# A weight-rounding pass in whole steps of 1024 columns, and xT casts on another engine, in an attention and feed-forward layer

## The reference

```python
# attention: 16 heads of 64
scores = q @ k^T * hs ** -0.5
p = softplus(scores) ** 2 * causal
out = (p / (sum(p, -1) + 1e-9)) @ v
x = layernorm(x + out @ w_proj^T + b_proj)

# feed-forward, d = 1024, f = 4096
def fake_quant_weight(w):
    scale = max(abs(w)) / 127
    return clip(round(w / scale), -128, 127) * scale
def qat_lora_linear(x, W, b, A, B):
    return x @ fake_quant_weight(W)^T + b + 2 * ((x @ A^T) @ B^T)
h = gelu(qat_lora_linear(x, W_fc, b_fc, A_fc, B_fc))
x = layernorm(x + qat_lora_linear(h, W_proj, b_proj, A_proj, B_proj))
```

## Time and profile before

| | us |
|---|---|
| median of 2 runs | 5843.04 |
| lowest and highest run | 5838.0, 5848.07 |
| the profiled execution | 5820.75 |
| its span, slowest core (core 7) | 5819.2 |
| spans of the 8 cores | 5794.4 to 5819.2 |

### The profile page before, as it was taken

One profiled execution on the slowest core, in us unless ns is written; L12 is line 12 of the kernel. 1 busy time (PEld: TensorE's weight loads), 2 busy tenths in 40 slices (PEclk: granted clock), 3 DMA queues, 4 the chain that ended last, 5 costly groups with the idle time before them and its releaser, 6 DMA issues. The chain is left out here.

```text
span 5819.2 us, 51500 instructions; the slowest of 8 cores (5794.4 to 5819.2 us)
## 1 busy us (share of the span) xinstructions
PE 3331.9 (57%) x12354; PEld 1140.0 (20%) x12354; DVE 1985.1 (34%) x3426; ACT 1831.0 (31%) x2257; POOL 233.0 (4%) x246
## 2 busy tenths in 40 slices
PE   0464555655665555556656620111478979888897
PEld 0121111111002211111110000000134434444343
DVE  2224333333333243333333345888821010111101
ACT  0005464655760053636647710000011111111111
POOL 0000101000001001010000000000000000000000
PEclk9975656555557856565555555555678888888888
DMA  3210101000001101010000025111100000000000
GB/s 83 78 57 14 48 9 48 6 7 33 5 6 52 58 20 50 9 47 7 7 33 5 6 89 183 55 56 56 62 15 30 15 30 15 15 30 15 30 15 15
DMA packets 91382, 205.94 MB, mean 35 GB/s; under 512 B 16823, under 2 KB 17080, under 8 KB 91100
## 3 DMA queue, kind: packets, MB, share of 16 engines
q1 hardware_dynamic: 81820, 169.09, 9.5%
q0 software_dynamic: 9280, 33.56, 1.4%
HBM read 168.79 MB, written 33.82 MB: 35 GB/s over the span
## 5 line engine op out<-in xcount | busy, mean ns | idle before, releaser
L551 DVE TENSOR_TENSOR a_p<-a_ph 128x1024 bf16<-128x1024 bf16 x640 | 445.4, 696 | 1319.5 <-ACT a_ph L548 1207.1
L543 ACT ACTIVATE a_tE<-psA 128x1024 f32<-128x1024 f32 x640 | 654.8, 1023 | 536.3 <-PE psA L533 505.7
L979 PE MATMUL psA<-b_Wp,b_h 128*128 128x512 bf16 x2048 | 581.5, 410 | 413.7 <-DVE b_Wp L816 392.1
L548 ACT ACTIVATE a_ph<-a_tE 128x1024 bf16<-128x1024 f32 x640 | 676.1, 1056 | 61.8 <-DVE a_p L551 2.8
L533 PE MATMUL psA<-a_Q,a_K 64*128 64x512 bf16 x1280 | 633.7, 596 | 2.2 <-DVE a_Q L474 2.2
L579 PE MATMUL psO<-a_p,a_V 128*65 128x512 bf16 x640 | 331.8, 621 | 519.0 <-DVE a_p L551 311.8
L579 PE MATMUL psU<-a_p,a_V 128*65 128x512 bf16 x640 | 315.0, 593 | 511.3 <-DVE a_p L551 272.6
L951 ACT ACTIVATE b_h<-psO,g_bfccol 128x256 bf16<-128x256 f32 x256 | 121.2, 473 | 1030.9 <-PE psO L943 1029.5
L1007 DVE TENSOR_SCALAR b_u<-psU 16x256 bf16<-16x256 f32 x16 | 6.6, 412 | 1106.3 <-PE psU L987 1106.3
L935 PE MATMUL psO<-b_X1T,b_Wfc 128*128 128x256 bf16 x2048 | 304.6, 298 | 89.2 <-DVE b_Wfc L816 76.6
L405 PE MATMUL psA<-a_xT,a_wqkv 128*128 128x512 bf16 x512 | 128.7, 418 | 335.6 <-POOL a_xT L309 335.6
(11 more groups left out here) (97 smaller groups left out, 3027.9 us busy)
## 6 DMA issues: line engine op xcount, KB each, us to landing
g_wstg<-xT SPq DMA_DIRECT2D x128, 256.0 KB
a_xf<-x SPq DMA_DIRECT2D x32, 512.0 KB
g_bc<-recb SPq DMA_DIRECT2D x128, 128.0 KB
x1scr<-g_xo POOLq DMA_DIRECT2D x32, 512.0 KB, 3.8
b_ws<-wfcT SPq DMA_DIRECT2D x32, 512.0 KB
b_ws<-wpF SPq DMA_DIRECT2D x32, 512.0 KB
b_x1f<-x1scr SPq DMA_DIRECT2D x32, 512.0 KB
b_ws<-wfcT SPq DMA_DIRECT2D x64, 256.0 KB
```

The costliest lines, as they stand in the source:

```text
L543: ve = kb.op("scalar", lambda E, pp=pp: E.activation(a_tE[:, :], psA[:, pp * 1024:(pp + 1) * 1024], AF.Exp, scale=0.125), waits=[(sPE, sco ...
L548: vl = kb.op("scalar", lambda E: E.activation(a_ph[:, :], a_tE[:, :], AF.Ln, bias=1.0), waits=[(sDV, st.get("ph_sq", 0))], inc=sAC)
L551: vsq = kb.op("vector", lambda E, pp=pp: E.tensor_tensor(a_p2[:, pp * 1024:(pp + 1) * 1024], a_ph[:, :], a_ph[:, :], ALU.mult), waits=[(sA ...
L979: kb.op("tensor", lambda E, q=q, tc2=tc2, oh=oh, pp=pp, f=f: E.matmul(psA[:, q * 512:(q + 1) * 512], b_h[:, pp * 256 + tc2 * 128: pp * 256 ...
```

## The change

It has two parts.

1. The second pass works on whole pieces. `emit_p2_step` takes the place of `emit_p2_half` and `halves`: one load of 128x1024 f32 (512 KB) into one of the two slots of `b_ws`, and the same seven instructions on 1024 columns, in `b_d`, `b_zi` and `b_r` from column 0. There are 64 steps in the same order: 8 of `b_Wfc`, 4 of `b_Wp`, three times, then 8 and the last 20. A load waits for the first operation of the step that used its slot before. The gates stand at the same places of the work.
2. The loads of xT for keys and values go through `load_xT`, so that VectorE does the 8 x 8 casts (before: GpSimd). The matmuls wait for VectorE's count. `load_xT_pool` stays for the queries of the later blocks, without its second argument.

```diff
-                    xtg_t = load_xT_pool(base + tg * 512, extra_waits=w + xw)
+                    xtg_ready = load_xT(base + tg * 512, extra_waits=w + xw)
                     for kf in range(CC):
                         bank = kf % 4
-                        w = [xtg_t, (sDV, st["psA_free"][bank])]
+                        w = [(sDV, xtg_ready), (sDV, st["psA_free"][bank])]
...
-            ws_free2 = [(sDV, ws_free[0]), (sDV, ws_free[0]),
-                        (sDV, ws_free[1]), (sDV, ws_free[1])]
-            qst = {"d_free": [0, 0], "rfin": [0, 0], "qi": 0, "first": True}
+            ws_free2 = [(sDV, ws_free[0]), (sDV, ws_free[1])]
+            qst = {"qi": 0, "first": True}
...
+            def emit_p2_step(which, src, dst, n):
                 sc = 4 * which
+                slot = qst["qi"] % 2
                 qst["qi"] += 1
+                vd = kb.dma("sync", lambda E, src=src, slot=slot, n=n: E.dma_start(
+                    out=b_ws[:, slot * 1024: slot * 1024 + n], in_=src),
+                    waits=[ws_free2[slot]])
+                wq = [vd]
                 if qst["first"]:
                     wq.append(scl_ready)
                     qst["first"] = False
+                vz = kb.op("vector", lambda E, slot=slot, n=n, sc=sc: E.tensor_scalar(
+                    b_d[:, 0:n], b_ws[:, slot * 1024: slot * 1024 + n],
                     g_scl[:, sc + 1:sc + 2], None, ALU.mult),
                     waits=wq, inc=sDV)
+                ws_free2[slot] = (sDV, vz)
+                kb.op("vector", lambda E, n=n: E.tensor_copy(
+                    b_zi[:, 0:n], b_d[:, 0:n]))
+                kb.op("vector", lambda E, n=n: E.tensor_copy(
+                    b_r[:, 0:n], b_zi[:, 0:n]))
+                kb.op("vector", lambda E, n=n: E.tensor_tensor(
+                    b_d[:, 0:n], b_d[:, 0:n], b_r[:, 0:n], ALU.subtract))
+                kb.op("vector", lambda E, n=n: E.scalar_tensor_tensor(
+                    b_r[:, 0:n], b_d[:, 0:n], 0.5, b_r[:, 0:n],
+                    ALU.is_ge, ALU.add))
+                kb.op("vector", lambda E, n=n: E.scalar_tensor_tensor(
+                    b_r[:, 0:n], b_d[:, 0:n], -0.5, b_r[:, 0:n],
+                    ALU.is_ge, ALU.add))
+                vfin = kb.op("vector", lambda E, dst=dst, n=n, sc=sc: E.tensor_scalar(
+                    dst, b_r[:, 0:n], g_scl[:, sc + 2:sc + 3],
                     g_scl[:, sc + 3:sc + 4], ALU.mult, ALU.add), inc=sDV)
                 return vfin
...
-                    for _ in range(16):
-                        vfin = emit_p2_half(0, *wfc_halves[fi])
+                    for _ in range(8):
+                        vfin = emit_p2_step(0, *wfc_steps[fi])
                         fi += 1
                     qfc_gate[hh] = vfin
-                    nwp = 8 if hh < 3 else 40
+                    nwp = 4 if hh < 3 else 20
                     for _ in range(nwp):
-                        if pi >= 64:
+                        if pi >= FC:
                             break
-                        vfin = emit_p2_half(1, *wp_halves[pi])
+                        wp_gate[pi] = emit_p2_step(1, *wp_steps[pi])
                         pi += 1
-                        if pi % 2 == 0:
-                            wp_gate[pi // 2 - 1] = vfin
```

More of the change, by code:

```diff
@@ L297, in load_xT, with load_xT_pool @@
                 return last
-            def load_xT_pool(t0, extra_waits=()):
+            def load_xT_pool(t0):
                 last = 0
@@ L306, in load_xT_pool @@
                         in_=d_xT[cc * 128:(cc + 1) * 128, t0:t0 + 512]),
-                        waits=[stg_state["free"][slot], (sPE, st["xT_rd"])] +
-                              (list(extra_waits) if cc == 0 else []))
+                        waits=[stg_state["free"][slot], (sPE, st["xT_rd"])])
                     vc = kb.op("gpsimd", lambda E, cc=cc, slot=slot: E.tensor_copy(
@@ L775, in build_program @@
                 waits=[vb1])
-            ws_free2 = [(sDV, ws_free[0]), (sDV, ws_free[0]),
-                        (sDV, ws_free[1]), (sDV, ws_free[1])]
-            qst = {"d_free": [0, 0], "rfin": [0, 0], "qi": 0, "first": True}
+            ws_free2 = [(sDV, ws_free[0]), (sDV, ws_free[1])]
+            qst = {"qi": 0, "first": True}
             qfc_gate = [0, 0, 0, 0]
             wp_gate = [0] * FC
-            QN = 512
-            def emit_p2_half(which, src, dst):
+            def emit_p2_step(which, src, dst, n):
                 sc = 4 * which
-                wslot = qst["qi"] % 4
-                p = qst["qi"] % 2
-                z0 = p * QN
+                slot = qst["qi"] % 2
                 qst["qi"] += 1
[L790 to L793, removed]
+                vd = kb.dma("sync", lambda E, src=src, slot=slot, n=n: E.dma_start(
+                    out=b_ws[:, slot * 1024: slot * 1024 + n], in_=src),
+                    waits=[ws_free2[slot]])
+                wq = [vd]
                 if qst["first"]:
@@ L796, in emit_p2_half @@
                     qst["first"] = False
-                vz = kb.op("vector", lambda E, wslot=wslot, z0=z0, sc=sc: E.tensor_scalar(
-                    b_d[:, z0:z0 + QN], b_ws[:, wslot * QN:(wslot + 1) * QN],
+                vz = kb.op("vector", lambda E, slot=slot, n=n, sc=sc: E.tensor_scalar(
+                    b_d[:, 0:n], b_ws[:, slot * 1024: slot * 1024 + n],
                     g_scl[:, sc + 1:sc + 2], None, ALU.mult),
                     waits=wq, inc=sDV)
-                ws_free2[wslot] = (sDV, vz)
@@ L818, in emit_p2_half @@
+                vfin = kb.op("vector", lambda E, dst=dst, n=n, sc=sc: E.tensor_scalar(
+                    dst, b_r[:, 0:n], g_scl[:, sc + 2:sc + 3],
                     g_scl[:, sc + 3:sc + 4], ALU.mult, ALU.add), inc=sDV)
-                qst["rfin"][p] = vfin
                 return vfin
[L822 to L827, removed]
@@ L829, in build_program @@
-            wfc_halves = halves(w_steps(0))
-            wp_halves = halves(w_steps(1))
+            wfc_steps = w_steps(0)
+            wp_steps = w_steps(1)
             def emit_p2_all():
```

## The result

The changed kernel took 5709.11 us (median of 11 runs, 5700.68 to 5818.8); the kernel before took 5859.01 us in 10 runs beside it. The ratio is 0.9798, 95% interval 0.9753 to 0.9843: 2.0% less, 118 us of 5859. The ratio compares fast runs alone; the two medians also hold slow ones, in which the cores of one die ran longer at a lower granted clock, so their quotient is not the ratio. The forecast was 5708 us and 135 us (2.3%) less. The time is where the forecast put it, but the saving, measured against the kernel before, is some 17 us smaller.

A forecast was written before the change was run, and what follows sets the result against it. VectorE's instruction chain was taken to bound the second pass; whole steps save 133.2 us (606.6 to 473.4) and VectorE casts 2, together 135 us, from the median 5843.04 to 5708 us. Range 5680 to 5726 us.

The forecast's parts named there:

- What bounds the kernel, and where a gain goes: Second pass: VectorE's chain paces the first tile's matmuls, so a microsecond off it starts the second tile a microsecond sooner.
- Part 1, the durations: Second pass: 1024-column instructions take 752, 693, 693, three times 1224, and 812 ns, 6.622 us busy per whole step.
- Part 1, the gaps: Second pass: 0.104 us ahead of each instruction, 0.728 us per step; half of 6 us of irregular gaps stays.
- Part 1, the covers: Second pass: loads, single buffers, TensorE and the second tile's b_x1f load stay hidden and do not pace the step.
- Part 2: Keys-and-values xT loads cast by VectorE: 2 us less, with bounds from 6 us less to 8 us more.
- The sum: Whole kernel: 133.2 + 2 = 135 us less, from the median 5843.04 to 5708 us, 2.3%.
- the tiles' length the same: Feed-forward tiles after the second pass: the same 1606 us at a granted clock of 0.86.
- faster by over 2%: Whole kernel: a saving beyond 2% (117 us), which needs the forecast case, given chance 0.83.
- The smaller fixed part: Rival, second pass: less fixed time per instruction than one-column rows say, 91 us saved half way, time 5750; chance 0.07.
- Casts and loads: Rival: VectorE casts cost 8 us and second-pass loads or gaps 13 us, time 5731; chance 0.06.
- The clock of the tiles: Rival, tiles: granted clock falls from 0.86 to 0.77, matmuls grow by 157 us, time 5865; chance 0.02.

The follow-up runs named there:

- e8: The kernel before with its second pass in 256 quarter steps of 256 columns, 128 KB loads into eight slots; 6134.27 us in one execution.
- e4: The kernel before, unchanged, measured a second time against itself; 5824.64 us, ratio 0.9977.
- e10: The kernel before with 450 idle one-column copies added to VectorE's list in the tile epilogues; 5826.98 us in one execution.
- e2: The kernel before with only the xT casts for keys and values moved to VectorE, half steps kept; 5815.09 us, ratio 0.9921.
- e6: The changed kernel with its 64 whole loads, but the seven instructions done twice on 512 columns; 5819.1 us in one execution.
- e9: The changed kernel with 450 idle one-column copies added to VectorE's list in the tile epilogues; 5672.73 us in one execution.
- e12: The changed kernel with 450 idle copies on VectorE, timed beside the unchanged changed kernel; 5690.25 us, ratio 0.9736 to the kernel before.
- e13: The changed kernel again, without idle copies, timed beside the one with 450 on VectorE; 5727.85 us, ratio 0.9793 to the kernel before.
- e15: The changed kernel with 450 idle copies on GpSimd instead of VectorE; 5756.76 us in one execution.
- e5: The changed kernel with each 512 KB load of the second pass cut into two of 256 KB, instructions kept whole; 5759.27 us in one execution.

## Why the prediction came out as it did

**What bounds the kernel, and where a gain goes.** Right. The second pass went from 606.65 to 472.5 us and the next tile came as much sooner; the projection blocks still wait, 3.1 to 3.4 us for the 3 forecast.

**Part 1, the durations.** Right within 1 ns for each kind. The two places where a size was taken from another kind (the one-tensor operations from L816 and L374, the two-tensor ones from one column) both held, and e8 carried the line to 256 columns. The Trainium skill's "VectorE: DVE Perf Modes", section on the TRN2 errata, has a formula for the f32 case with two tensors, (N + 151) cycles at 0.96 GHz: 690.6, 1224 and 424 ns for N of 512, 1024 and 256. By that, the rows agree with it (692, 1225, 425), and not with the 58 cycles of the table in the same section.

**Part 1, the gaps.** Right for the regular ones (0.104 us). For the irregular ones the size was nearly right and the reason wrong: the prediction let half of 6 us stay, 3 us, "since half the instructions do"; 4 of 16 gaps stayed, 1.4 us, and what decides is where every 128th entry of the list falls. So the stage gave 134.1 us and not 133.2.

**Part 1, the covers.** All held. The loads were not waited for; the b_x1f load was issued at 4098.19, 20.6 us before the end (21 forecast).

**Part 2.** The sign was right and the size too small. The forecast took 2 us less, out of bounds from 6 us less to 8 us more. Averaged over executions of the short band, keys and values 1 take 188.2 us with the casts on GpSimd (the kernel before, e4, e10) and 185.4 on VectorE (e2, e6, e9, e12), 2.8 us less, which is the 4 x 0.186 x 4 = 3 us of the casts on the chain. The waits before the second sequence's groups are 77.5 to 82.3 us against 73.9 to 78.3 on four cores of each, 4 us less in the mean (80.0 and 76.0). That is 7 us; the stage lengths of all these executions keep apart, while the waits of single cores overlap a little. The error was to give the two VectorE loads of the earlier trace rows (17.4 and 19.0 us) more weight than the durations: they stand at another place, and two loads are too few against a jitter of 1 us.

**The sum.** Here it failed. It added the edited terms and left all other stages at their old length, with the tiles "the same 1606 us". The edited terms alone, corrected, come to about 141 us. e12, with the first pass in the short band, shows 5665.7 us of span against 5806.6, 140.9 us less; that the two agree so well is chance, since e12's start is 8 us longer than that of the kernel before and its tiles 5 us shorter, and by its ratio of 0.9736 it saves 154 us. In the changed kernel unedited stages took some 24 us more by the table (7.0 + 2.9 + 9.7 + 4.3). The start's 7.0 us lies within the scatter between executions; most of the rest comes back with the idle copies. So the 118 us measured are, as far as the stages show, 141 less what stages lost that no line of the diff touches: the step that failed is "the tiles' length the same", and with it the term of zero for every stage outside the edit, which measured some 24 us. The 0.83 for "faster by over 2%" had no room for that: the ratios 0.9798, 0.9760 and 0.9793 all lie just under 0.98, and the interval of each reaches over it. That the time of 5709 us met the 5708 forecast is luck: by the ratio of 0.9798, the forecast's own starting point of 5843.04 us leads to 5725 us.

**The rivals.** The smaller fixed part fell with the 1225 ns. Casts and loads took nothing back. The clock of the tiles is 0.87 on the undisturbed core; no loss there that would be the change's. What came true, a loss of some 0.4% in stages outside the edit (24 of 5807 us in the table), was not among them.

**What stays open.** That idle instructions at the end of VectorE's list shorten stages ahead of them is shown by e12 against e13. That it is VectorE's list and not the whole program's rests on e15, one execution, which has as many instructions as e12. Since e8 is long again, it is not simply the length, and why it happens is not shown. The loads of wpF are slower though they are issued the same way, which points to memory or the path to it, but that is only argued; the place of the program or of the data in memory was neither seen nor changed on purpose. The instruction queue moves 1.25 MB in e13 and 1.30 MB in e12, and also 1.30 MB in e15, whose first pass is long, so it isn't the amount that is fetched. The Trainium skill's "Runtime: NRT & Kernel Launch", section "Instruction fetch mechanics", says that each engine fetches its instructions in 16 KiB blocks over a DMA queue and that this is mostly hidden. Here the packets of q14 have 8192 bytes, and 0.46 us of gap go with some of them on VectorE; no run shows whether they have a part in the longer stages.

## What to carry to other kernels

On a chain of small VectorE instructions count the instructions: here each f32 one carries a fixed time of about 160 ns (two tensor inputs, or a cast) to 280 ns (a scale with two per-row scalars, 812 - 2 x 266) and 0.1 us of gap, and one form measured at two lengths in the profile gives the price of a third to a nanosecond. Then ask whether fewer instructions do the same work, which was worth more than three times as much as longer ones (7.5% in all against 2%). And when a saving read from the profile doesn't arrive in full, add up all stages of both profiles, the unedited ones too, and time a copy with idle instructions before looking for a cause in the edit.

## What the runs showed of the hardware

450 idle copies at the end of VectorE's instruction list moved this kernel by 38 us (0.7%), e13 to e12, in stages that run before them: the load-bound first pass, where seventeen executions form two bands and no gradual change, and attention. The same copies on GpSimd did not do it (e15). The other surprise is smaller: in the seven-operation second pass every gap of 0.46 us in VectorE's chain, in place of 0.10, stands at a distance of 128 list entries or a multiple from the next, waits counted, on all cores (16 in the kernel before, 32 in e8, 7 in e6, 4 in the changed kernel), and none shows in e5, where the 128th entry is always a wait. Neither the number nor the size of the loads moves them.
